# Buffers of a weight matrix split into high and low halves: four split blocks and four raw ones instead of five and two

## The chip, the cores and the metric

The kernel runs on one core of a Trainium2 chip. The metric is the device time of one execution in microseconds (us); lower is better. The engines are named as the profile names them: PE is TensorE, DVE is VectorE, ACT is ScalarE, POOL is GpSimd and SP is SyncE, which here only starts transfers.

## What is computed

A table of 12500 items with 512 numbers each, 1024 users with 200 item ids each. For each user the table's rows of all valid ids (below 12500) are averaged, and the average is multiplied by a 512 x 12500 matrix W; a bias is added. In the reference, cut to what matters:

```
valid = sequence_ids < emb_table.shape[0]
seq_emb = emb_table[where(valid, sequence_ids, 0)] * valid[..., None]
denom = maximum(valid.sum(axis=1, keepdims=True), 1.0)
user_repr = seq_emb.sum(axis=1) / denom
logits = user_repr @ proj_w + proj_b
```

Most ids are invalid: they are drawn up to 109962, so a user has some 23 valid ones.

## The kernel before, in words

**Tiles.** The users are 8 tiles t of 128 (TILES). W is cut into 25 blocks of 500 columns, each 512 x 500 floats, 1000 KB, held as four pieces of 128 rows. A *unit* is one product: one user tile by one block of W, into one of six banks of PSUM (BANKS). Each factor is split into a high part that PE takes exactly in fp32r and a low rest, and a unit is 4 pieces x 3 products (high by high L649, high by low L650, low by high L651), 12 matmuls. There are 200 units.

**Blocks of W.** A block passes through `load_w` (SP, L194 to L197: one transfer into one of RAW buffers w_raw), `w_high` (ACT, L298 to L302: the rounded copy w_hi) and `w_low` (DVE, L473 to L479: the rest w_lo, in two instructions L476 and L478). w_hi and w_lo have SPLIT buffers. A load may start when w_lo of the block RAW earlier is made (L196). `w_high(q)` waits until the last product with block q - SPLIT is done (L300).

**Means.** For every user tile, DVE sorts the ids (`sort`, L378), POOL starts 26 indirect gathers (FAST) of one table row per user, called columns here, into a ring of 12 row buffers (ROWS), and one more gather for rests. Before a gather, ACT sets two row buffers to zero (`clear`, L286 to L296), which must wait until the two columns that lay there were added. The columns of tiles 0 and 1 are added by PE (`sum_column`, L605), those of tiles 2 to 7 by DVE (`add_column`, L421). DVE then forms the mean (`mean_of`, L453 to L466), PE transposes it (`turn`, L582, matmul L587), ACT and DVE split it (`mean_high` L304, `mean_low` L468).

**Order of the work.** The means come one after the other while products already run, so user tile t joins late: at load q = JOIN[t] (0, 8, 12, 15, 18, 20, 22, 24). When it joins, it first catches up on the blocks still on chip, SPLIT - 1 before load q, and then shares every further block. `start[t]` (L44) is the first block of tile t; what it missed is loaded again at the end, so there are LOADS = start[-1] + 25 loads. L46 to L58 write the list of units and from it first_unit and last_unit of each block and joined[t], the first unit of tile t. With SPLIT = 5: LOADS = 45 and joined = 0, 8, 20, 33, 49, 63, 79, 97. With SPLIT = 4 the same lines give LOADS = 46 and joined = 0, 8, 19, 31, 46, 59, 74, 91.

Every engine runs one loop over the units r. Two rules set what goes between:

```
split_due = [None] * SPLIT + [min(last_unit[q - SPLIT] + 1, first_unit[q] - 1) for q in range(SPLIT, LOADS)]
begin, end = (joined[t - 1] - MEAN_AHEAD + 1, joined[t] - SUM_AHEAD) if t >= ON_PE else (2, joined[t] - 2)
return begin + (end - begin) * j // (FAST - 1)
```

The first (L71) gives the unit at which block q is split: DVE does w_low(q) after moving out unit split_due[q], ACT does w_high(q) one unit earlier, and ahead of that unit's clears (L346 to L360). The second (L65 to L69, `column_due`) spreads the 26 columns j of tile t over the units ahead of its joining. For tile 1 (units 2 to 6, the same at either SPLIT) it gives columns 0 to 6 at unit 2, 7 to 12 at unit 3, 13 to 18 at unit 4, 19 to 24 at unit 5 and 25 at unit 6. Column 24 goes into the buffer that column 12 left, and the clear of that pair (12, 13) stands in ACT's list at unit 4. `mean_of(t)` stands on DVE after unit joined[t] - 3, `turn(t)` on PE before unit joined[t] - 1.

DVE also moves every unit out of PSUM and adds the bias (`move_out`, L481 to L490, instruction L489); a unit of PE waits until the unit six before it was moved. SP stores one or two units at a time.

The last due times, for the blocks that matter here. SPLIT = 5: blocks 5, 6, 7, 8 at units 1, 2, 3, 4, block 9 at 9. SPLIT = 4: blocks 4, 5, 6, 7, 8 at units 1, 2, 3, 4, 5, block 9 at 9. Before the first mean, ACT and DVE split blocks 0 to SPLIT - 1 (L331 to L337 and L536 to L555), and SP loads blocks 0 to SPLIT + RAW - 1, the first RAW of them without a wait (L213 to L218).

Of the kernel before, what the change touches and what calls it, by code (L numbers as in the profile page):

```python
# [5 lines left out]
def mean_embedding_projection(nc, ids, table, proj, bias, out, FAST=26,  # L6
# [17 lines left out]
    REST = SORTED - FAST  # L24
    REST_AT = 18
    LISTED = -(-FAST // TOP) * TOP
    RAW, SPLIT, BIAS, ROWS, PLACED, BANKS = 2, 5, 4, 12, 2, 6
    CH = 2
    ON_PE = 2
    COLS = FAST * TILES  # L30
# [23 lines left out]
    UNITS = len(units)  # L54
    assert UNITS == TILES * NB
    first_unit = [min(r for r, (x, _) in enumerate(units) if x == q) for q in range(LOADS)]
    last_unit = [max(r for r, (x, _) in enumerate(units) if x == q) for q in range(LOADS)]
    joined = [min(r for r, (_, x) in enumerate(units) if x == t) for t in range(TILES)]  # L58
    stores, at = [], 0
    for q, first, n in steps:  # L60
# [18 lines left out]
    with ctx:  # L79
# [283 lines left out]
        def _(dve):  # L363
# [14 lines left out]
            def sort(t, r):  # L378
                at = SORT_OPS * t
                if r == 0:  # L380
                    keys(key[:], t, s_sort, at)
                eight = top[:, t, TOP * r:TOP * (r + 1)]
                dve.max(eight, key[:]).then_inc(s_sort, 1)  # L383
                dve.wait_ge(s_sort, at + KEY_OPS + 2 * r + 1)
                dve.tensor_scalar(index[:, t, TOP * r:TOP * (r + 1)], eight, -1.0, float(ITEMS),
                                  ALU.mult, ALU.add).then_inc(s_index, 1)
                dve.match_replace(key[:], eight, key[:], -1.0).then_inc(s_sort, 1)  # L387
                dve.wait_ge(s_sort, at + KEY_OPS + 2 * r + 2)
# [64 lines left out]
            def mean_of(t):  # L453
                if t >= ON_PE:
                    dve.wait_ge(s_summed, FAST * (t + 1 - ON_PE))
                else:
                    if t:
                        dve.wait_ge(s_mean, t)
                    dve.memset(sums[:], 0.0).then_inc(s_cleared, 1)
                    dve.wait_ge(s_cleared, t + 1)  # L460
                add_further(t)
                if t:
                    dve.wait_ge(s_turned, t)
                dve.wait_ge(s_rest_mean, t + 1)
                dve.scalar_tensor_tensor(mean[:], sums[:], inv_count[:, t:t + 1], rest_mean[:], ALU.mult,  # L465
                                         ALU.add).then_inc(s_mean, 1)  # L466
# [6 lines left out]
            def w_low(q):  # L473
                dve.wait_ge(s_w_hi, q + 1)
                half = K // 2
                dve.tensor_tensor(w_lo[:, q % SPLIT, 0:half], w_raw[:, q % RAW, 0:half],  # L476
                                  w_hi[:, q % SPLIT, 0:half].bitcast(F32), ALU.subtract)
                dve.tensor_tensor(w_lo[:, q % SPLIT, half:], w_raw[:, q % RAW, half:],  # L478
                                  w_hi[:, q % SPLIT, half:].bitcast(F32), ALU.subtract).then_inc(s_w_lo, 1)  # L479
# [72 lines left out]
            w_low(3)  # L552
            for r in range(ROUNDS):
                sort(3, r)
            w_low(4)  # L555
            mean_of(0)
            mean_low(0)
            for r in range(UNITS):
# [116 lines left out]
```

## Time and profile before

| | |
|---|---|
| median of 3 runs | 692.52 us (692.03 to 693.82) |
| profiled execution, its own time | 696.46 us |
| its span, first to last instruction | 694.7 us |
| mean granted clock of PE | 0.963 of full speed |
| busy: PE, DVE, ACT, POOL | 628.5, 402.5, 206.4, 225.1 us |
| transfers | 157.61 MB, 227 GB/s over the span |
| chain that ended last, by engine | PE 69%, DVE 15%, DMA 6%, issue 6%, ACT 2% |

The span is shorter than the execution by what lies around it, 1.8 us. "Busy" is a sum over the whole span, in which the stages differ: in the first 53 us there is no product, until 409 us user tiles join one by one, and from there on only products run. In the timeline's rows the first number is the start in us, the second the duration, and brackets hold the idle time of the engine ahead of the instruction and what ended it. The waits' rows give the idle time in all, how many times, and the longest.

### The profile page before, as it was taken

How to read it: one execution, taken by the hardware profiler on the slowest of the kernel's cores; microseconds unless marked ns; L12 is line 12 of the kernel's file. 1: busy time of each engine (PE TensorE's matmuls, PEld its weight loads, DVE VectorE, ACT ScalarE, POOL GpSimd, SP SyncE). 2: the span in 40 equal slices, each digit the busy share in tenths (PEclk: the TensorE clock that was granted, in tenths of full speed). 3: DMA queues.
4: the chain of work that ended last, by engine and by line, in shares of the span. 5: the costliest groups of instructions: out<-in, count | busy, mean ns of one | idle time of the engine just before them, and what ended most of it. 6: DMA issues, size and time to landing. Idle time of an engine off the chain costs nothing.

```text
span 694.7 us, 7435 instructions
## 1 busy us (share of the span) xinstructions
PE 628.5 (90%) x2596; PEld 492.3 (71%) x2596; DVE 402.5 (58%) x733; ACT 206.4 (30%) x182; POOL 225.1 (32%) x227
## 2 busy tenths in 40 slices
PE   1968669974988998989999999999999999999998
PEld 0425336863866877868878878888888888888886
DVE  7973114987896988968658546433233444334342
ACT  6543243353554344335333022111111111112110
POOL 6773456456376376665736100000000000000000
PEclk9998879996997999999999999999999999999999
DMA  8976748798988988988869328745545555665753
GB/s 309 332 234 211 245 159 269 232 342 263 274 291 265 295 293 274 304 285 286 283 196 320 140 101 271 217 153 175 173 160 167 173 168 166 184 211 183 221 148 104
DMA packets 76251, 157.61 MB, mean 227 GB/s; under 512 B 8168, under 2 KB 63592, under 8 KB 76208
## 3 DMA queue, kind: packets, MB, share of 16 engines
q1 hardware_dynamic: 58928, 109.63, 47.9%
q0 software_dynamic: 17280, 47.47, 21.9%
q8 instruction: 20, 0.33, 0.2%
q14 instruction: 23, 0.19, 0.1%
HBM read 115.04 MB, written 51.20 MB: 239 GB/s over the span
## 4 chain that ended last, share of the span: by engine, by line
PE 69%; DVE 15%; DMA 6%; issue 6%; ACT 2%; DVEq 1%; POOL 0%; POOLq 0%; ACTq 0%
PE acc L651 22%; PE acc L649 21%; PE acc L650 21%; DVE sums L429 5%; PE turned L613 3%; DMA w_raw<-in_L_rec_proj_w_dram 3%; DMA rows<-in_L_rec_emb_table_dram,index 3%; DVE w_lo L478 2%; DVE w_lo L476 1%; DVE key L387 1%; ACT w_hi L302 1%; DVE top L383 1%; PE turned L587 1%; DVE stage L489 1%; DVEq L190 1%
## 5 line engine op out<-in xcount | busy, mean ns | idle before, releaser
L649 PE MATMUL acc<-w_hi,mean_hi 128*128 128x500 f32 x800 | 321.6, 402 | 1.4 <-DVE mean_lo L470 1.4
L651 PE MATMUL acc<-w_hi,mean_lo 128*128 128x500 f32 x800 | 317.6, 397 | 0.0
L650 PE MATMUL acc<-w_lo,mean_hi 128*128 128x500 f32 x800 | 314.9, 394 | 0.0
L489 DVE TENSOR_TENSOR stage<-acc,bias_sb 128x500 f32<-128x500 f32 x200 | 134.9, 676 | 237.2 <-PE acc L651 236.8
L252 POOL DMA_INDIRECT rows<-in_L_rec_emb_table_dram,index x208 | 215.6, 1036 | 155.9 <-ACT rows L295 85.9
L650 PEld LDWEIGHTS acc<-w_lo,mean_hi 128*128 128x128 f32 x800 | 153.5, 192 | 36.5 <-issue 3.2
L649 PEld LDWEIGHTS acc<-w_hi,mean_hi 128*128 128x128 f32 x800 | 153.5, 192 | 35.6 <-issue 3.2
L651 PEld LDWEIGHTS acc<-w_hi,mean_lo 128*128 128x128 f32 x800 | 152.8, 191 | 31.4
L302 ACT ACTIVATE w_hi<-w_raw 128x2000 fp32r<-128x2000 f32 x45 | 84.4, 1876 | 297.0 <-PE acc L651 258.8
L295 ACT ACTIVATE rows<-zero 128x1024 f32<-128x1024 f32 x104 | 107.2, 1050 | 112.4 <-DVE sums L429 88.7
L429 DVE TENSOR_TENSOR sums<-sums,rows 128x512 f32<-128x512 f32 x150 | 104.2, 695 | 6.1
L613 PE MATMUL turned<-rows,ident 128*128 128x512 f32 x104 | 52.8, 657 | 18.1 <-DMA rows<-in_L_rec_emb_table_dram,index 16.8
L476 DVE TENSOR_TENSOR w_lo<-w_raw,w_hi 128x1000 fp32r<-128x1000 f32 x45 | 53.8, 1196 | 11.5 <-ACT w_hi L302 11.4
L478 DVE TENSOR_TENSOR w_lo<-w_raw,w_hi 128x1000 fp32r<-128x1000 f32 x45 | 53.8, 1195 | 0.0
L613 PEld LDWEIGHTS turned<-rows,ident 128*128 128x128 f32 x104 | 21.0, 208 | 45.1 <-DMA rows<-in_L_rec_emb_table_dram,index 22.6
L587 PE MATMUL turned<-ident,mean 128*128 128x128 f32 x32 | 6.6, 340 | 29.6 <-DVE mean L465 29.6
L587 PEld LDWEIGHTS turned<-ident,mean 128*128 128x128 f32 x32 | 4.3, 169 | 33.1 <-DVE mean L465 33.0
L465 DVE SCALAR_TENSOR_TENSOR mean<-sums,inv_count,rest_mean 128x512 f32<-128x512 f32 x8 | 6.0, 751 | 18.6 <-issue 13.1
L383 DVE MAX8 top<-key 128x8 f32<-128x200 f32 x40 | 14.6, 366 | 0.8
L387 DVE MATCH_REPLACE8 key<-top,key 128x200 f32<-128x200 f32 x40 | 14.2, 355 | 0.0
L323 ACT ACTIVATE rest_mean<-turned,inv_count 128x512 f32<-128x512 f32 x8 | 5.4, 676 | 24.0 <-PE turned L603 19.8
L306 ACT ACTIVATE mean_hi<-turned 128x512 fp32r<-128x512 f32 x8 | 4.8, 598 | 23.4 <-PE turned L587 23.4
(67 smaller groups left out, 96.9 us busy)
## 6 DMA issues: line engine op xcount, KB each, us to landing
w_raw<-in_L_rec_proj_w_dram SPq DMA_DIRECT2D x45, 1000.0 KB, 6.0
out_dram<-stage SPq DMA_DIRECT2D x73, 500.0 KB, 4.4
out_dram<-stage SPq DMA_DIRECT2D x54, 250.0 KB, 3.3
bias_sb<-in_L_rec_proj_b_dram SPq DMA_DIRECT2D x45, 250.0 KB, 5.1
rows<-in_L_rec_emb_table_dram,index POOLq DMA_INDIRECT x208, 4.8
ids_sb<-in_r_sequence_ids_dram SPq DMA_DIRECT2D x1, 700.0 KB, 4.6
rest_rows<-in_L_rec_emb_table_dram,rest_index POOLq DMA_INDIRECT x8, 6.7
ids_sb<-in_r_sequence_ids_dram SPq DMA_DIRECT2D x1, 100.0 KB, 2.1
```

What stands on the lines that cost most here:

```text
L252: return pool.indirect_dma_start(out=dst, out_offset=None, in_=table, in_offset=bass.IndirectOffsetOnAxis(ap=column, axis=0), bounds_check ...
L295: nc.scalar.activation(rows[:, c % ROWS:c % ROWS + CH].rearrange("p c d -> p (c d)"), zero[:, 0:1].to_broadcast([P, CH * HID]), ACT.Copy). ...
L302: nc.scalar.activation(w_hi[:, q % SPLIT], w_raw[:, q % RAW], ACT.Copy).then_inc(s_w_hi, 1)
L383: dve.max(eight, key[:]).then_inc(s_sort, 1)
L429: dve.tensor_tensor(sums[:], sums[:], rows[:, c % ROWS], ALU.add).then_inc(s_summed, 1)
L476: dve.tensor_tensor(w_lo[:, q % SPLIT, 0:half], w_raw[:, q % RAW, 0:half], w_hi[:, q % SPLIT, 0:half].bitcast(F32), ALU.subtract)
L478: dve.tensor_tensor(w_lo[:, q % SPLIT, half:], w_raw[:, q % RAW, half:], w_hi[:, q % SPLIT, half:].bitcast(F32), ALU.subtract).then_inc(s_ ...
L489: dve.tensor_tensor(stage[:, g % STAGE, r - stores[g][0]], acc[:, r % BANKS, 0:BW], bias_sb[:, q % BIAS], ALU.add).then_inc(s_moved, 1)
L613: nc.tensor.matmul(turned[:], ident[:], rows[:, c % ROWS], start=j == 0, stop=j == FAST - 1).then_inc(s_added, 1)
L649: nc.tensor.matmul(bank, hi, high, start=k == 0, stop=False)
L650: nc.tensor.matmul(bank, hi, low, start=False, stop=False)
L651: last = nc.tensor.matmul(bank, lo, high, start=False, stop=k == K - 1)
```

## The change

Of the buffers, w_raw has four instead of two and w_hi and w_lo have four instead of five. A raw block takes 8 KB of a partition and a split one 16 KB, so both layouts take 96 KB. The split of block 4 ahead of the first mean is taken out of DVE's list; ACT's list follows from SPLIT, and so do the list of units, the due times and the number of loads.

```diff
-    RAW, SPLIT, BIAS, ROWS, PLACED, BANKS = 2, 5, 4, 12, 2, 6
+    RAW, SPLIT, BIAS, ROWS, PLACED, BANKS = 4, 4, 4, 12, 2, 6
...
             w_low(3)
             for r in range(ROUNDS):
                 sort(3, r)
-            w_low(4)
             mean_of(0)
             mean_low(0)
```

## Rows read from the trace of the kernel before

**Rows 1.** Windows from mean to mean: stretch, busy us (instructions), clock, DMA share, GB/s

```profile
0.00:53.09 53.09, 30.88 (x63) 12.88 (x63) 42.99 (x145) 30.44 (x29) 38.43 (x45) 0.97 0.86 294
...
116.85:165.42 48.57, 35.80 (x161) 29.06 (x159) 41.20 (x79) 23.14 (x22) 26.31 (x26) 0.90 0.88 285
```

**Rows 2.** Timeline of PE: the first transpose of the means of tiles 2, 3, 4, 5, 7

```profile
166.23 0.48 PE L587 MATMUL turned<-ident,mean 128*128 128x128 f32 x1 [13.58 <-DVE mean L465]
...
211.62 0.48 PE L587 MATMUL turned<-ident,mean 128*128 128x128 f32 x1 [6.22 <-DVE mean L465]
...
262.43 0.33 PE L587 MATMUL turned<-ident,mean 128*128 128x128 f32 x1 [2.26 <-DVE mean L465]
...
305.09 0.33 PE L587 MATMUL turned<-ident,mean 128*128 128x128 f32 x1 [2.47 <-DVE mean L465]
...
406.26 0.33 PE L587 MATMUL turned<-ident,mean 128*128 128x128 f32 x1 [1.02 <-DVE mean L465]
```

**Rows 3.** Waits of DVE in the stages of tiles 2, 3, 4, 6, 7, in turn

```profile
DVE w_lo L476 <- ACT w_hi L302: 2.0, 2, 1.1
...
DVE w_lo L476 <- ACT w_hi L302: 1.8, 1, 1.8
...
DVE w_lo L476 <- ACT w_hi L302: 1.3, 1, 1.3
...
DVE stage L489 <- PE acc L651: 10.5, 9, 2.2
...
DVE stage L489 <- PE acc L651: 14.0, 12, 2.4
```

**Rows 4.** Windows: units 97 to 199 (4 instructions of L650 a unit), of that line alone

```profile
409.48:691.40 281.92, 160.20 (x412) 77.62 (x412) 1.00 0.57 179
```

**Rows 5.** Timeline of ACT: the split of block 8, then clears

```profile
89.37 1.87 ACT L302 ACTIVATE w_hi<-w_raw 128x2000 fp32r<-128x2000 f32 x1 [11.30 <-PE acc L651]
91.15 5.76 ACT L295 ACTIVATE rows<-zero 128x1024 f32<-128x1024 f32 x6
```

**Rows 6.** Timeline of POOL: the gather of column 18 of tile 1

```profile
93.06 1.00 POOL L252 DMA_INDIRECT rows<-in_L_rec_emb_table_dram,index  x1 [7.20 <-ACT rows L295]
```

**Rows 7.** Timeline of PE: columns and starts of units 4 and 5 (two records a column)

```profile
99.27 2.08 PE L613 MATMUL turned<-rows,ident 128*128 128x512 f32 x2 [5.64 <-DMA rows<-in_L_rec_emb_table_dram,index]
100.36 1.41 PE L649 MATMUL acc<-w_hi,mean_hi 128*128 128x500 f32 x1
...
105.63 5.31 PE L613 MATMUL turned<-rows,ident 128*128 128x512 f32 x12
110.38 0.79 PE L649 MATMUL acc<-w_hi,mean_hi 128*128 128x500 f32 x1
```

**Rows 8.** Windows: units 32, 48, 62 (each after a join's wait), of L650 alone

```profile
212.39:217.54 5.15, 2.47 (x4) 1.33 (x4) 0.50 0.90 283
...
262.84:265.65 2.81, 1.55 (x4) 0.76 (x4) 1.00 0.84 270
...
305.50:309.87 4.37, 2.24 (x4) 1.08 (x4) 0.61 0.86 288
```

**Rows 9.** Timeline of DVE: the mean of tile 1; units 32 and 46 moved out

```profile
116.85 0.75 DVE L465 SCALAR_TENSOR_TENSOR mean<-sums,inv_count,rest_mean 128x512 f32<-128x512 f32 x1 [1.82 <-ACT rest_mean L323]
...
217.85 0.68 DVE L489 TENSOR_TENSOR stage<-acc,bias_sb 128x500 f32<-128x500 f32 x1 [2.35 <-PE acc L651]
...
257.48 0.68 DVE L489 TENSOR_TENSOR stage<-acc,bias_sb 128x500 f32<-128x500 f32 x1 [0.62 <-PE acc L651]
258.08 0.69 DVE L429 TENSOR_TENSOR sums<-sums,rows 128x512 f32<-128x512 f32 x1
```

**Rows 10.** The chain that ended last, by pieces, in the stage of tile 3

```profile
179.91 1.12 DVE w_lo L478
...
181.04 6.81 DMA w_raw<-in_L_rec_proj_w_dram
...
187.94 1.89 ACT w_hi L302
```

## The prediction

> **What bounds the kernel now.** I first cut the span where DVE forms a mean, since that is where the stages end; a window from one mean to the next shows which engine is full in it [rows 1]. Then I looked at PE ahead of each transposed mean: how long it stood, and for whom [rows 2]. Then at what DVE itself waited for between two means [rows 3], and at the stretch behind the last joining [rows 4].
>
> The reader is to see three regimes. Until the mean of tile 0 there is no product. From there to the last joining PE waits at every join for a mean of DVE: 13.58 us for tile 2, then 6.22, 2.26, 2.47 and, for tile 7, 1.02 [rows 2]. In the stages of tiles 2 to 5 DVE is the bound: it hardly waits for a product. In those of tiles 6 and 7 it waits for products 10.5 and 14.0 us [rows 3], so PE is the bound, and the small wait left at the join is the fixed way from unit joined - 3 through the last column to the mean. Behind the last joining only products run: 103 units in 281.92 us, 2.74 us each, with no gap [rows 4].
>
> So the end is the time of the mean of tile 7 plus all units not yet done by then. This is the ledger that I keep.
>
> **Part 1: what the list of units does.** Joins come at 8, 19, 31, 46, 59, 74, 91 instead of 8, 20, 33, 49, 63, 79, 97: the first stage keeps its 8 units and each of the six others loses one, since a tile catches up on three blocks, not four. The 200 units stay. Thus 6 units move behind the last joining: 6 x 2.74 = **+16.4 us** there. What must pay for them is a shorter way to each of the six means.
>
> **Part 2: stages of tiles 6 and 7, bound by PE.** Each loses a unit of PE: 2 x -2.74 = **-5.5 us**. DVE can follow: it has 10.5 and 14.0 us of waiting, and the stage shrinks for it by 2.74 less the 0.60 of one unit moved out.
>
> **Part 3: stages of tiles 2 to 5, bound by DVE.** DVE has the same 26 columns, sorts and splits in each (4, 3, 3 and 2 blocks fall due in them under either list), and one unit less to move out: from start to start 0.60 us [rows 9]. Besides, DVE's waits for a split whose block was late go away: 2.0, 1.8 and 1.3 us for tiles 2, 3, 4 [rows 3]; with four raw buffers the block of each split was asked for four splits earlier, many units before. Tile 4's stage also had a wait of 0.62 for product 46 [rows 9], which a PE one unit ahead takes away. That gives -2.6, -2.4, -2.5 and -0.6: **-8.1 us**. PE gets 2.74 earlier to each of these joins, so its wait there grows: nearly nothing for tiles 2 to 4, by 2.1 us for tile 5 (from 2.47 to 4.6). ACT's own waits for loads hide behind DVE's columns, which never wait for a gather in these stages, so they are worth nothing more.
>
> **Part 4: the stage of tile 1.** Its 8 units stay, and it isn't a matter of DVE: PE adds the columns itself and waits for gathers. Read the round at unit 3: ACT's split of block 8 has to wait for product 3 and starts at 89.37, the clears stand behind it (91.15) [rows 5], POOL's gather behind these at 93.06 [rows 6], it lands at 99.27 and unit 4 starts at 100.36 [rows 7]. From product to unit 10.99 us, though the columns alone need under 5. There are two such rounds, at units 2 and 3, because splits stand there ahead of clears. At unit 4 no split stood in ACT's list, and the next columns ran through: from 105.63 to unit 5 at 110.38 [rows 7]. Now block 8 moves to due time 5, that is to unit 4 of ACT, behind product 4 (it reuses block 4's buffers) and ahead of the clear that column 24 needs. So a third round: unit 5 starts at 105.83 + 10.99 = 116.8 instead of 110.38, **+6.4 us**. From below this is 0 (if the gather were early enough after all), from above 11.0; I take the value of the equal round just ahead of it. Then the clock: unit 4, behind a wait of 5.64, took 5.27 us (100.36 to 105.63) [rows 7] against 2.74 for a full-speed unit, so up to +2.5; unit 62, behind a shorter wait, took 4.37 [rows 8], so +1.6 from below. I take **+2.0**. Last, DVE splits block 8 behind unit 5, now ahead of the mean of tile 1: two instructions, of which the second takes 1.12 [rows 10], 2 x 1.12 = **+2.2 us**. The 1.82 us that DVE stood ahead of this mean [rows 9] could hide most of it; but the same pause stands ahead of other means whose sums are long ready, so it is the loading of registers, and the split comes on top. From below 0.4, from above 2.2. Sum of the stage: **+10.6 us**.
>
> **Part 5: before the first mean.** ACT's and DVE's split of block 4 goes, and two more loads (2 MB) are asked for at the start. At 294 GB/s two loads are 7.0 us of transfer. POOL's gathers follow each other there and PE's last columns wait for the last of them; DVE is done early. The loads could delay the first gathers by up to 7.0, or make the later ones faster because block 6's load has gone ahead. The first columns are no end of a chain, so I take **0**, from -1 to +2.3 (a third of the 7.0, as PE starts late on the first columns).
>
> **Part 6: the clock at joins.** Unit 32, behind a wait of 6.22, ran at 0.50, unit 48 behind 2.26 at 1.00, unit 62 behind 2.47 at 0.61 [rows 2, 8]. Tile 5's join will have 4.6 us of waiting: its next unit goes from 4.37 towards 5.15, **+0.8**. What tiles 2 to 5 lose otherwise is hidden in PE's waits. The Trainium skill (TensorE: Matmul & The Clock Gate, section "HAM oscillation — how this bites in real kernels") says that waits ahead of each piece of work let PE's clock fall to half each time, 1.2 instead of 2.4 GHz; by that rule tile 4's unit would be slow too, which at 2.26 us this trace does not show (clock 1.00); what it would cost is in the second rival.
>
> **Part 7: one more load, split and its parts.** 46 blocks instead of 45: the extra one falls behind the last joining, where DVE and ACT wait for PE, and has five units, 13.7 us, between due and use: nothing. Three stores fewer: nothing. If that cover were gone, 1.9 of ACT and 2.2 of DVE.
>
> **Sum.** 16.4 - 5.5 - 8.1 + 10.6 + 0 + 0.8 = **+14.2 us**. The profiled execution took 696.46 us (span 694.7 and 1.8 around it); by its own time the new one would take 710.7. It stands 3.9 us above the median of 692.52, so in terms of the median: **706.7 us**, slower by 2.1%.
>
> **Rivals.**
> - *No third round.* If the gather of column 24 is in time (ACT free early, or the clear not last), the 6.4 and 2.0 fall away: 706.7 - 8.4 = **698.3**. For it: other columns of unit 5 give 4.3 us of cover. Against: the rounds at units 2 and 3 have the same cover and stood.
> - *The clock and the early loads cost more.* If tile 4's join now also slows the next unit, DVE, which has few columns to do there, waits for it as it does for unit 32, 2.35 us [rows 9]; with the 2.3 of part 5: **711.4**.
> - *The loads of W were the bound* (the other side: not slower). The chain that ended last runs in tile 3's stage through a load of 6.81 and a split of 1.89 on ACT [rows 10]. Were these 8.7 us all to go from the way to the mean, instead of the 1.8 that DVE waited, stage 3 would gain until its PE has no more to wait, 5.5; stage 2 likewise 8.7 - 2.0 = 6.7; stage 4, where PE waits 2.5, some 1.5: 706.7 - 13.7 = **693.0**. It decides where DVE would have been done with everything ahead of that split. Against: DVE's own wait is 1.8, and it was busy 41.2 of 48.6 us in stage 2 [rows 1]. The Trainium skill (DMA: Bandwidth & Descriptors, section "Rules for kernel authors") says to issue a transfer early and wait late; that rule speaks for this case.
>
> **How the numbers follow.** The sum's case has 0.66, no third round 0.12, more clock and loads 0.11, loads as the bound 0.06; 0.05 is left for something unseen that makes it faster. A difference of 0.3% (2.1 us) is about what a measurement of this kernel can tell from none. Faster 0.05, same 0.06, slower 0.89. The range reaches from the case without a third round to the dear one: 698 to 712.
>
> **What would show it.** Right: the last joining comes at unit 91, with 109 units of 2.74 behind it; a third wait of PE of over 5 us for a gather, at about 110; splits on DVE that never wait for ACT; the mean of tile 1 some 10 us later, the gap of means 6 and 7 shorter by 2.7 each. Wrong: stages 2 to 5 shorter by more than 2.7 us each, or the stage of tile 1 unchanged. If stage 2 alone shrinks by 9 us, the chain of waits was right about the loads and I was not.

## The result, and the profile after

The changed kernel took 703.12 us (702.43 to 705.42, 4 runs) beside 693.17 us (692.03 to 694.47) for the kernel before: ratio 1.0149, 95% interval 1.0118 to 1.0179. It is slower by 1.5%, some 10 us. Its profiled execution took 703.12 us with a span of 701.4, the one of before 696.46 with 694.7; so the two traces differ by 6.7 us, and the profile of before happened to lie 3.3 us above its own median. On a later occasion all times were longer, and there the same change was faster; that is told with the experiments.

First the windows from mean to mean, cut as in [rows 1], now at the means of tiles 0 to 7 of the changed kernel (columns: the stretch, then its length, busy us of PE, PEld, DVE, ACT, POOL with their instructions, PE's clock, DMA share, GB/s):

```profile
0.00:51.19 51.19, 29.76 (x63) 11.35 (x63) 40.56 (x143) 28.92 (x28) 37.14 (x44) 1.00 0.94 331
51.19:123.02 71.83, 53.26 (x147) 32.46 (x147) 18.31 (x26) 24.09 (x23) 31.72 (x32) 0.83 0.62 193
123.02:168.84 45.82, 31.96 (x143) 26.00 (x143) 40.43 (x78) 22.44 (x21) 29.87 (x28) 0.91 0.92 320
168.84:212.84 44.00, 36.89 (x155) 30.02 (x155) 38.62 (x77) 20.78 (x20) 26.38 (x25) 0.89 0.85 285
212.84:260.54 47.70, 45.22 (x191) 36.92 (x191) 40.50 (x80) 20.90 (x20) 28.55 (x28) 0.94 0.89 288
260.54:301.48 40.94, 37.36 (x167) 30.52 (x167) 36.92 (x75) 19.04 (x19) 26.46 (x27) 0.99 0.90 290
301.48:348.79 47.31, 45.24 (x191) 36.95 (x191) 33.51 (x53) 19.25 (x19) 30.36 (x30) 0.94 0.86 282
348.79:398.01 49.22, 48.20 (x215) 39.53 (x215) 34.25 (x53) 12.50 (x12) 16.70 (x17) 1.00 0.62 209
398.01:701.40 303.39, 299.07 (x1324) 248.24 (x1324) 121.38 (x155) 40.03 (x22) 0.00 (x0) 1.00 0.54 170
```

The ledger of the prediction can be read off by subtracting the same stretches of before, whose means stand at 53.09, 116.85, 165.42, 210.82, 261.62, 304.29, 353.31 and 405.45 us:

| stretch | before | after | difference | forecast |
|---|---|---|---|---|
| to the mean of tile 0 | 53.09 | 51.19 | -1.9 | 0 |
| stage of tile 1 | 63.76 | 71.83 | +8.1 | +10.6 |
| tile 2 | 48.57 | 45.82 | -2.8 | -2.6 |
| tile 3 | 45.40 | 44.00 | -1.4 | -2.4 |
| tile 4 | 50.80 | 47.70 | -3.1 | -2.5 |
| tile 5 | 42.67 | 40.94 | -1.7 | -0.6 |
| tiles 6 and 7 | 101.16 | 96.53 | -4.6 | -4.7 |
| behind the mean of tile 7 | 289.25 | 303.39 | +14.1 | +16.4 |
| sum | 694.7 | 701.4 | +6.7 | +14.2 |

The forecast of tiles 6 and 7 is -5.5 of part 2 and the +0.8 of the clock behind tile 5's join, whose unit lies in that stretch.

The mean of tile 1 is 6.2 us later than before (123.02 for 116.85), that of tile 4 already 1.1 earlier and that of tile 7 7.4 earlier; then 6 more units stand behind it.

The third round of the stage of tile 1 is there. In the timeline of the changed kernel, ACT's split of block 8, the clear behind it, POOL's gather of column 24 and PE's wait for it (the lines of the changed file are one lower from L555 on: L612 is the old L613, L648 the old L649):

```profile
103.39 1.87 ACT L302 ACTIVATE w_hi<-w_raw 128x2000 fp32r<-128x2000 f32 x1 [11.59 <-PE acc L650]
105.17 1.04 ACT L295 ACTIVATE rows<-zero 128x1024 f32<-128x1024 f32 x1
...
107.06 0.99 POOL L252 DMA_INDIRECT rows<-in_L_rec_emb_table_dram,index  x1 [8.78 <-issue]
...
112.39 1.54 PE L612 MATMUL turned<-rows,ident 128*128 128x512 f32 x2 [4.74 <-DMA rows<-in_L_rec_emb_table_dram,index]
112.95 1.40 PE L648 MATMUL acc<-w_hi,mean_hi 128*128 128x500 f32 x1
```

It is the chain of [rows 5 to 7] once more, one unit later: from the split at 103.39 to unit 5 at 112.95 it is 9.56 us, where the round of unit 4 took 10.99. The split waited 11.59 us for its product, and the gather behind it landed 5.33 us after its start (6.21 in the round of unit 4).

PE's waits at the joins of tiles 2, 3, 4, 5 and 7, as in [rows 2]:

```profile
169.64 0.47 PE L586 MATMUL turned<-ident,mean 128*128 128x128 f32 x1 [13.86 <-DVE mean L465]
...
213.64 0.47 PE L586 MATMUL turned<-ident,mean 128*128 128x128 f32 x1 [7.11 <-DVE mean L465]
...
261.34 0.33 PE L586 MATMUL turned<-ident,mean 128*128 128x128 f32 x1 [2.48 <-DVE mean L465]
...
302.29 0.47 PE L586 MATMUL turned<-ident,mean 128*128 128x128 f32 x1 [3.59 <-DVE mean L465]
...
398.82 0.33 PE L586 MATMUL turned<-ident,mean 128*128 128x128 f32 x1 [1.03 <-DVE mean L465]
```

They were 13.58, 6.22, 2.26, 2.47 and 1.02. PE loses a unit in each stage and DVE's way to the mean shrinks by nearly as much, except in the stage of tile 5. DVE's waits in the stage of tile 2 (line, what it waited for, us in all, times, longest) no longer name a split:

```profile
DVE mean L465 <- issue: 4.4, 2, 2.8
DVE mean_lo L470 <- ACT mean_hi L306: 0.8, 1, 0.8
```

### The profile page after: what moved, and what is told of

Read it like the earlier page. It is cut to its first block, busy times and chain, and to the rows that moved or that the text cites. A ratio compares the mean times of both kernels' runs of the same rounds, so it can differ in the third digit from the quotient of the medians.

```text
span 701.4 us, 7435 instructions
## 1 busy us (share of the span) xinstructions
PE 627.0 (89%) x2596; PEld 492.0 (70%) x2596; DVE 404.5 (58%) x735; ACT 208.0 (30%) x183; POOL 227.2 (32%) x227
## 3 DMA queue, kind: packets, MB, share of 16 engines
q1 hardware_dynamic: 59552, 110.91, 47.4%
## 4 chain that ended last, share of the span: by engine, by line
PE 62%; DVE 18%; issue 10%; DMA 4%; POOL 2%; ACT 2%; DVEq 2%; POOLq 0%
PE acc L648 20%; PE acc L649 19%; PE acc L650 19%; DVE sums L429 8%; DMA rows<-in_L_rec_emb_table_dram,index 4%; DVE w_lo L476 2%; DVE w_lo L478 2%; POOL rows L252 2%; PE turned L612 2%; ACT rows L295 1%; DVE key L387 1%; DVE stage L489 1%; PE turned L586 1%; DVEq L190 1%; DVE mean L465 1%
## 5 line engine op out<-in xcount | busy, mean ns | idle before, releaser
L648 PE MATMUL acc<-w_hi,mean_hi 128*128 128x500 f32 x800 | 323.1, 404 | 1.4 <-DVE mean_lo L470 1.4
L649 PE MATMUL acc<-w_lo,mean_hi 128*128 128x500 f32 x800 | 315.1, 394 | 0.0
L650 PE MATMUL acc<-w_hi,mean_lo 128*128 128x500 f32 x800 | 314.5, 393 | 0.0
L648 PEld LDWEIGHTS acc<-w_hi,mean_hi 128*128 128x128 f32 x800 | 154.0, 193 | 35.7 <-issue 3.2
L649 PEld LDWEIGHTS acc<-w_lo,mean_hi 128*128 128x128 f32 x800 | 153.8, 192 | 33.6 <-issue 3.5
L650 PEld LDWEIGHTS acc<-w_hi,mean_lo 128*128 128x128 f32 x800 | 153.0, 191 | 31.9
L302 ACT ACTIVATE w_hi<-w_raw 128x2000 fp32r<-128x2000 f32 x46 | 86.2, 1874 | 297.5 <-PE acc L650 296.4
L612 PE MATMUL turned<-rows,ident 128*128 128x512 f32 x104 | 53.2, 648 | 21.7 <-DMA rows<-in_L_rec_emb_table_dram,index 20.3
L478 DVE TENSOR_TENSOR w_lo<-w_raw,w_hi 128x1000 fp32r<-128x1000 f32 x46 | 55.1, 1197 | 0.0
L476 DVE TENSOR_TENSOR w_lo<-w_raw,w_hi 128x1000 fp32r<-128x1000 f32 x46 | 54.9, 1193 | 0.1
L612 PEld LDWEIGHTS turned<-rows,ident 128*128 128x128 f32 x104 | 19.7, 201 | 49.9 <-DMA rows<-in_L_rec_emb_table_dram,index 31.6
L323 ACT ACTIVATE rest_mean<-turned,inv_count 128x512 f32<-128x512 f32 x8 | 5.4, 677 | 26.6 <-PE turned L602 17.9
```

Of the source, the lines that this page charges most:

```text
L302: nc.scalar.activation(w_hi[:, q % SPLIT], w_raw[:, q % RAW], ACT.Copy).then_inc(s_w_hi, 1)
L612: nc.tensor.matmul(turned[:], ident[:], rows[:, c % ROWS], start=j == 0, stop=j == FAST - 1).then_inc(s_added, 1)
L648: nc.tensor.matmul(bank, hi, high, start=k == 0, stop=False)
L649: nc.tensor.matmul(bank, hi, low, start=False, stop=False)
L650: last = nc.tensor.matmul(bank, lo, high, start=False, stop=k == K - 1)
```

## Experiments

Twelve runs were made: groups of four, four and three, and one alone, each group on one chip beside the kernel before. In the three groups the kernel before took 742.3, 735.1 and 739.7 us on the median, and beside the last run 728.4, not 693: the same program in a different setting. Ratios are to the kernel before of the same group.

**The kernel before once more**, for a trace of that setting.

> The kernel before, unchanged, for a second trace. My theory of the result: the first profile of before was some 3 us above its own median, and part of the shift by stages (mean of tile 0 at 53.1 against 51.2 us after the change) is scatter and not the change. Expected here: first mean at 51 to 53 us, units 97 to 199 again 2.74 us each. Rival: the first mean is always at 53.1 before the change, and its 1.9 us gain comes from the earlier loads and the split that left; then it stands at 53.1 here too.

It took 743.7 us, with the mean of tile 0 at 61.86. Units 97 to 199 took 2.736 us each, as before. What is longer stands ahead of the last joining. In its timeline, PE in the middle of a product, and DVE moving the unit ahead of it:

```profile
277.63 0.39 PE L650 MATMUL acc<-w_lo,mean_hi 128*128 128x500 f32 x1 [1.66 <-issue]
...
279.78 0.58 PE L651 MATMUL acc<-w_hi,mean_lo 128*128 128x500 f32 x1 [1.76 <-issue]
...
284.79 0.68 DVE L489 TENSOR_TENSOR stage<-acc,bias_sb 128x500 f32<-128x500 f32 x1 [11.39 <-remote]
```

PE's matmuls, otherwise 0.23 us apart, start 2.1 us apart, with 1.7 us of idle time between them and nothing that they wait for ("issue"), and DVE stands for 11.39 us with a releaser that is in none of this core's queues ("remote"), while POOL starts a gather every 1.30 us. I call these standstills. The three longest of DVE in this trace (11.4, 7.5 and 4.9 us) all end 2.4 to 2.8 us after the last gather of an unbroken row of POOL (that row ends at 282.1, 335.6 and 231.2 us); in the first trace of before POOL has such rows too, some of 20 gathers and more, without a standstill, so the rows alone don't make them. By the same cut as above, this run is longer than the first trace of before by 8.8 us ahead of the first mean and by 5.1, -0.7, 4.4, 13.6, 9.6, 4.0 and 2.4 in the seven stages, and by nothing behind them: 47.2 us. Neither theory on the first mean is tested by that, since it came even later than 53.1.

**The changed kernel in that setting.**

> The changed kernel, unchanged, beside the others of this call and a run of before on the same chip. In the call before this one the kernel before took 742 us, not 693, and its vector engine and PE stood still at places where the profile names no releaser in the core. Theory: in a calm setting the change costs 1.3 to 1.7%, as first measured; where those standstills are there, it goes by them and the sign may turn (variants of it ran at 725 against 742). Rival: the change always costs about 10 us, also where before takes 742.

It took 725.96 us, ratio 0.9891 (0.9821 to 0.9962): faster. Its windows for the stages of tiles 1, 4 and behind the last mean:

```profile
58.94:132.53 73.59, 54.43 (x147) 33.20 (x147) 18.41 (x26) 23.62 (x22) 29.12 (x29) 0.82 0.57 179
...
222.59:278.40 55.81, 46.79 (x191) 37.48 (x191) 40.62 (x80) 21.02 (x20) 30.45 (x31) 0.87 0.84 273
...
422.73:726.10 303.37, 299.07 (x1324) 248.26 (x1324) 121.38 (x155) 40.04 (x22) 0.00 (x0) 1.00 0.55 170
```

The last stretch is the same as in the first setting to 0.02 us, so the price of the 6 units is a fixed one. The standstills are there too, but the trace lost less to the setting: 726.1 - 701.4 = 24.7 us against the 47.2 of the kernel before. (These two traces are of different groups; by the medians within a group the kernel before lost 42 and 47 us, 735.1 and 739.7 for 693.2, and the changed kernel 23, 726.0 and 726.4 for 703.1.) In the stage of tile 4 it lost 8.1 us to the setting (55.81 for 47.70), the kernel before 13.6 (64.43 for 50.80). The difference, 22.5 us by the traces and 19 to 23 by the medians, is more than the 10 by which the change was slower: the sign turns.

**And once more.**

> The changed kernel beside the two below, for a third occasion. Theory: the ratio to before goes with the setting: 1.015 where before takes some 693 us, 0.98 to 0.99 where it takes 735 to 742 because the vector engine and PE stand still in the stages of tiles 0 and 4 to 7. Rival: it was drift between calls, and the ratio is on either side whatever before takes.

726.39 us, 0.9842 (0.9763 to 0.9920), beside 739.7. So far the ratio goes with the setting: 1.015 where before takes 693, below 1 where it takes 735 or 740. The first kind was met on one occasion only, so that half isn't repeated.

**Split blocks alone**: four of them, but two raw ones.

```diff
-    RAW, SPLIT, BIAS, ROWS, PLACED, BANKS = 4, 4, 4, 12, 2, 6
+    RAW, SPLIT, BIAS, ROWS, PLACED, BANKS = 2, 4, 4, 12, 2, 6
```

> Only one half of the change: four split blocks, but still two raw ones. Theory: the list of units and the third round before unit 5 come from the split blocks alone (units 4 to 5 again 15 us, 10 in the kernel before); the raw ones give back only what the vector engine waited for late blocks, 2.0 + 1.8 + 1.3 = 5.1 us. So 703.1 + 5.1 = 708 us. Rival 1: the loads of W were the bound of stages 2 to 4 and four raw buffers gave some 14 us: 717 us. Rival 2: raw buffers are worth nothing: 703 us.

736.95 us, 0.9969 (0.9918 to 1.0020). Units 4 to 5 took 16.3 us: the third round comes from the split blocks, as does the list of units. The kernel with four of both and w_raw elsewhere, in the same group (below), took 724.92, so two more raw blocks are worth 12.0 us in that setting, where I had 5.1. The two traces differ by more, 17.9 us. The stages of tiles 2 and 3 make 2.3 and 2.8 us of that, near the 2.0 and 1.8 of the prediction's part 3, though DVE's waits for a split in them are only 0.4 and 2.2; the stage of tile 4 makes 8.4 (63.24 against 54.87), by standstills that the trace does not tie to a load. All twelve traces of this setting bear the last one out: the stage of tile 4 takes 63.2 to 66.4 us in the five with two raw blocks (four of these with five split blocks, one with four) and 53.9 to 55.8 in the seven with four raw blocks. So that gain goes with the raw blocks, whichever the number of split ones. It is not the whole of the turned sign: with four split and two raw blocks the kernel is already no slower than before here (0.9969), and its stages of tiles 6 and 7 are 6.3 and 5.3 us shorter than those of the kernel before once more, where the first pair gave 1.7 and 2.9. In this setting "the loads of W were the bound" comes near in size (13.7); what it forecast for the stage of tile 2, 6.7 us less, is not there.

**The third round undone**: in ACT's list at unit 4 the split stands behind the clears.

```diff
                 for q in range(SPLIT, LOADS):
-                    if split_due[q] == r + 1:
+                    if split_due[q] == r + 1 and not (r == 4):
                         w_high(q)
...
                         clear(g + ring)
+                for q in range(SPLIT, LOADS):
+                    if split_due[q] == r + 1 and r == 4:
+                        w_high(q)
```

> The changed kernel with one step moved: in the scalar engine's list at unit 4 the split of block 8 stands behind the clears, not ahead of them. Theory: the third wait for a gather (4.74 us ahead of the last column of unit 5) goes, with the slow clock behind it: units 4 to 5 take 10 us instead of 15.2, unit 5 1.7 us less, so 703.1 - 6.8 = 696.3 us, and the mean of tile 1 comes that much earlier. Rival: the gather itself was late for another reason (full transfer queues), and the wait stays: 703.1.

724.99 us, against 724.92 for the kernel of the same group that keeps the round (the one with other places in memory, below). The round is gone: in this trace the last of the columns, the next unit, and then DVE moving unit 5:

```profile
115.02 1.02 PE L615 MATMUL turned<-rows,ident 128*128 128x512 f32 x2
115.48 0.80 PE L651 MATMUL acc<-w_hi,mean_hi 128*128 128x500 f32 x1
...
123.46 0.68 DVE L492 TENSOR_TENSOR stage<-acc,bias_sb 128x500 f32<-128x500 f32 x1 [9.56 <-PE acc L653]
```

Units 4 to 5 took 10.0 us and PE waited for no gather there (there: 16.0). But product 5 was done at 118.6, and DVE moved it only at 123.46: a standstill of some 5 us took the gain. The run shows the cause of the round, not its price.

**The same again.**

> The same kernel as in the earlier call, where the third wait for a gather went (units 4 to 5: 10.0 against 16.0 us in its sister) but the time did not fall, since the vector engine then stood still for some 5 us ahead of the mean of tile 1 with no releaser. Theory: without such a standstill the whole falls by the 6.8 us of the third round, against the changed kernel of this call. Rival: something else holds the mean of tile 1, and the time stays within 2 us of the changed kernel's.

725.2 us against 725.96 of the changed kernel in the group; units 4 to 5 in 8.7 us instead of 14.9, and again DVE stood still ahead of the mean of tile 1 (11.3 us "remote" in this stage). The rival has it by the time, in this setting alone; the four runs spread from 716 to 730 us, so a gain of some us would be hard to see. What the round costs without a standstill is shown only by the first pair of traces.

**Other places in memory**: w_raw allocated behind w_lo instead of ahead of w_hi.

```diff
-        w_raw = sb("w_raw", [P, RAW, K, BW], F32)
         w_hi = sb("w_hi", [P, SPLIT, K, BW], F32R)
         w_lo = sb("w_lo", [P, SPLIT, K, BW], F32R)
+        w_raw = sb("w_raw", [P, RAW, K, BW], F32)
```

> The changed kernel with the same work, only w_raw placed behind w_hi and w_lo in the memory, so that both of these lie 32000 bytes lower. In the traces a unit takes 2.72 to 2.75 us before the change, by which buffer its block lies in, and 2.70 to 2.73 after it. Theory: the place of w_hi and w_lo sets this, so the times per buffer change here (by 0.01 to 0.05 us each, and the whole by up to 200 x 0.03 = 6 us either way). Rival: it goes by something else (the number of buffers, what else runs), and units stay at 2.71 on the mean and the whole at 703.1.

724.92 us, and units as in the changed kernel to 0.001 us: 2.714, 2.708, 2.700 and 2.729 for the four buffers. The place as such changes nothing. But in the run with two raw blocks, where w_hi begins 16000 bytes lower, the same four times come rotated by two buffers: 2.700, 2.728, 2.714, 2.709. A buffer is 8000 bytes, that is 64 more than a whole number of 256. A shift of four buffers (32000, a whole number of 256) changes nothing and one of two buffers (128 more than such a number) rotates the times by two, so they fit the start's remainder by 256. What differs between four and five buffers is that with five the matching w_lo starts 40000 bytes behind w_hi, 64 off.

**That distance, in the kernel before**: the stage buffers (24000 bytes) between w_hi and w_lo, which makes it 64000.

```diff
         w_hi = sb("w_hi", [P, SPLIT, K, BW], F32R)
+        stage = sb("stage", [P, STAGE, GROUP, BW], F32)
         w_lo = sb("w_lo", [P, SPLIT, K, BW], F32R)
         bias_sb = sb("bias_sb", [P, BIAS, BW], F32)
-        stage = sb("stage", [P, STAGE, GROUP, BW], F32)
```

> The kernel before with the same work, only the stage buffers placed between w_hi and w_lo in the memory, so that w_lo lies 64000 bytes behind w_hi and not 40000. In all traces with four split blocks w_lo lies 32000 bytes behind w_hi, a whole number of 256, and a unit takes 2.713 us on the mean, wherever the pair lies; with five the distance is 64 bytes off such a number and it takes 2.736. Theory: the distance sets it, and units 97 to 199 take 2.71 here, 200 x 0.023 = 4.6 us less over all or at least the 2.4 of the last stretch. Rival: it goes by the number of split blocks, and they stay at 2.74.

The windows of the units behind the last joining, of the instructions of L649 alone (stretch, length, PE and PEld busy, clock, DMA share, GB/s). The kernel before, its units 97 to 199:

```profile
409.48:691.40 281.92, 160.07 (x412) 77.22 (x411) 1.00 0.57 179
```

The same 103 units with the stage buffers between:

```profile
454.10:733.30 279.20, 160.06 (x412) 77.20 (x411) 1.00 0.58 180
```

2.710 us a unit instead of 2.736, with five split blocks. By buffer they take 2.700, 2.729, 2.714, 2.709 and 2.700 us, the times of the run with two raw and four split blocks, where w_hi starts at the same place, with the fifth like the first; before it was 2.752, 2.727, 2.726, 2.720 and 2.748. So the distance sets it, not the number of blocks, and it gives 2.7 us here. (The step also moves the stage and bias buffers, but from the kernel before to the changed one these stay where they were and the unit still goes from 2.736 to 2.713.) The whole took 738.36, ratio 1.0037 (0.9957 to 1.0117): too small to be seen in that setting.

**Splits behind clears in the kernel before**, in the whole stage of tile 1 (the diff of the third round with `r < joined[1]` for `r == 4`).

> The kernel before (five split blocks, two raw), with one step moved: in the stage of tile 1 the scalar engine's splits stand behind its clears. Theory: the rounds of product, split, clear, gather at units 2 and 3 go as the third one does; both waits of PE for a gather (5.7 and 5.6 us) and the slow clock behind them vanish, units 2 to 5 take some 8.5 us each instead of 14.4, 15.9 and 10.0, so 12 to 15 us less than the kernel before. Rival: the gathers are then paced by their own issue (1.30 us each) or their landing and PE waits as before: 0 to 3 us less.

726.22 us, 0.9882 (0.9822 to 0.9941). PE waits for no gather any more; units 2 to 5 start 7.9 us apart, and the stage takes 47.7 us instead of the 68.9 of the kernel before once more. By the medians within the group 9 us arrive, between the theory's 12 to 15 and the rival's 3. Against the trace once more, which is of another group, 17 us are left (741.9 to 724.9): the next stage takes back 3.5, and every other is within 1.1. The group has no trace of the kernel before itself, so where the rest of its gain goes is not shown.

**The same in the changed kernel.**

> The changed kernel with the scalar engine's splits behind its clears in the whole stage of tile 1. In the kernel before, this step took the stage from 68.9 to 47.7 us. Theory: here all three waits for a gather go, the stage falls from some 73 to 48 us and the whole by 18 to 25 us against the changed kernel (some comes back in the next stage, where the clears then have no lead): about 703 us where the changed kernel takes 726, 682 where it takes 703. Rival: the next stages take it all back, since the gathers then bound them: within 5 us of the changed kernel.

707.03 us, 0.9585 (0.9506 to 0.9664) of before, 0.973 of the changed kernel in its group. Its windows for the stages of tiles 1 and 2:

```profile
58.09:109.51 51.42, 46.78 (x147) 29.21 (x147) 18.28 (x26) 24.05 (x22) 26.26 (x26) 0.91 0.71 226
109.51:156.60 47.09, 33.75 (x143) 27.12 (x143) 40.65 (x77) 22.31 (x21) 32.73 (x30) 0.88 0.95 340
```

And PE's columns ahead of units 3, 4 and 5, which follow their unit without a wait:

```profile
78.87 5.31 PE L615 MATMUL turned<-rows,ident 128*128 128x512 f32 x12
...
86.75 5.31 PE L615 MATMUL turned<-rows,ident 128*128 128x512 f32 x12
...
94.61 5.31 PE L615 MATMUL turned<-rows,ident 128*128 128x512 f32 x12
```

The stage of tile 1 falls from 72.8 us to 51.4 in the group, and the next one keeps its length (47.4 and 47.1). 19.4 us arrive. So the three rounds together, not the work of splitting W, which is still there, were the large cost of this stage. This version beats both kernels in this setting; in the one of the first pair it wasn't run.

**Both steps in the kernel before.**

> The kernel before with both steps: splits behind clears in the stage of tile 1, and the stage buffers between w_hi and w_lo. Theory: they add up, 9 to 17 us of the first and 2 to 5 us of the second: 0.965 to 0.985 of the kernel before, units 97 to 199 at 2.71 us each. Rival: the second is lost in standstills, as when it stood alone (1.004): 0.98 to 0.99 and still 2.71 us a unit in the last stretch.

715.61 us, 0.9719 (0.9630 to 0.9808), units at 2.710 us. In this setting five split blocks with both steps stay behind four with one; the stage of tile 4 alone is 65.3 us against 55.0, as in the other traces with two raw blocks against four.

**The split of block 8 behind the mean**, on top of the best version.

```diff
                 for q in range(SPLIT, LOADS):
-                    if split_due[q] == r:
+                    if split_due[q] == r and r != joined[1] - MEAN_AHEAD:
                         w_low(q)
...
                     mean_of(joined.index(r + MEAN_AHEAD))
+                for q in range(SPLIT, LOADS):
+                    if split_due[q] == r and r == joined[1] - MEAN_AHEAD:
+                        w_low(q)
```

> The changed kernel with the splits behind the clears in the stage of tile 1 (0.9585 of before in the last call), and besides the vector engine's split of block 8 behind the mean of tile 1, not ahead of it. Theory of the prediction: this split costs 2.2 us ahead of that mean, so the way from the move of unit 5 to the mean gets 2.2 us shorter, and the whole by up to 2 us: about 0.955 of before. Rival: the split stood beside a wait for registers and products and costs nothing there, or comes back ahead of the next mean, whose stage the vector engine bounds (then the first way is 2.2 shorter, the next stage 2.2 longer, and the ratio stays at 0.958).

704.69 us, 0.9670 (0.9616 to 0.9723), beside a kernel before of 728.4; the ratio can't be held against the 0.9585 of another setting, so on the whole this is open. The way is clear from the traces: from the start of unit 6 to the mean of tile 1 it is 3.0 us instead of 5.7, which is the 2.2 of the split and 0.5 that was not traced, and the next stage is 47.3 instead of 47.1, so nothing is taken back there.

## Why the prediction was right, and where its terms were off

It forecast 706.7 us and a range of 698 to 712; measured were 703.1. The sign, the mechanism and the order of the terms held in the setting that it was made for: 6 units behind the last joining, a third round in the stage of tile 1, and six shorter ways to a mean that don't pay for them. The size is less well met than the 3.6 us between 706.7 and 703.1 say. The ledger compares two traces, and there 14.2 us were forecast and 6.7 measured, with most terms too dear. The forecast for the median comes nearer because it takes off the 3.9 us by which the trace of before lay above its median; those us lie somewhere in the stages of that trace, and part of what the ledger missed is them (1.7 are found below, ahead of the first mean). By its steps:

- **The units behind the last joining**: 16.4 forecast, 14.1 measured. The number of units was right. The duration was not the same on both sides: I took 2.74 us for all 109, and they take 2.71, since the distance of w_lo from w_hi changed with the number of buffers. 109 x 0.023 = 2.5 us. No row of before could say that; but durations from 2.72 to 2.75 by buffer were to be seen and I had averaged over them.
- **The third round**: 6.4 forecast, 5.1 measured (units 4 to 5 in 15.16 us instead of 10.02), mostly as this gather landed 0.9 us sooner; the wait for it was 4.74 us, a little under the "over 5" that was to show it. The clock behind it: 2.0 against 1.7 (unit 5 to 6: 6.07 for 4.42). The split of block 8 ahead of the mean: 2.2 against 2.0 (from unit 6 to the mean 4.0 us instead of 2.05), so it did come on top of DVE's pause, which is still 1.56. The rounds at units 2 and 3 were 0.5 us shorter besides.
- **Stages of tiles 2 to 4**: 7.5 forecast, 7.3 measured. DVE's waits for a split are gone. Tile 3's stage gave 1.0 less, of which 0.5 is DVE's longer wait for the slow unit behind the join of tile 2 (0.91 for 0.41). "Shorter by more than 2.7 each" was to show the forecast wrong: tiles 2 and 4 pass it narrowly (2.8 and 3.1), tiles 3 and 5 don't (1.4 and 1.7).
- **Stage of tile 5**: 0.6 forecast, 1.7 measured; PE's wait is 3.59 and not 4.6. Of the 1.1 more, 0.3 is the loading of registers; the rest was not traced.
- **The clock at the joins**: behind 2.48 us of waiting the transpose took 0.33 us, as before behind 2.26; behind 3.59 it took 0.47, as one at the lower level does. So tile 4's join kept its clock (its unit took 2.80 us), against the second rival. The unit behind tile 5's join took 4.85 us for 4.36, so the 0.8 is 0.5. Waits of 2.47 us, before, and 2.48, after, lie on either side: the first let the clock fall within the unit, the second didn't, and no run here says why. The rule of the Trainium skill that the prediction set beside it (TensorE: Matmul & The Clock Gate, "HAM oscillation — how this bites in real kernels") agrees with the traces at waits of 3.59 us and more here, not at 2.48. The prediction put that rule more widely than the page does, whose kernel waits longer than tile 4's join at each step; so this join does not speak against the page.
- **Before the first mean**: 0 forecast, 1.9 us less measured. The range went to -1. Both chains run through the same gather, started at 39.44 us before and 39.23 after, so 0.2 is that. The rest is PE's last columns and the product between them: before, behind a wait of 3.58 us, they ran at the lower level (granted clock 0.68 from 45.99 to 51.39 us), after, behind one of 1.42, at full clock (1.00 over the same stretch). Whether the change or scatter made the waits shorter is open: in the other setting the first mean comes at 52.2 to 61.9 us in the five traces with two raw blocks and at 57.2 to 61.4 in the seven with four.
- **The rivals**: no third round and the dear clock did not come. Loads as the bound: by the first pair of traces no, stage 2 gained 2.8 and not 9.

What the prediction did not have at all is the setting. Its numbers stand on a kernel at 693 us; at 735 to 740 us the change is 1.1 to 1.6% faster, because the setting costs it 19 to 23 us less. That the loss is smaller with four raw blocks is shown for the stage of tile 4 (8.4 us in one group, with no overlap between the five traces with two raw blocks and the seven with four); what starves PE and DVE there is open. The groups ran on different chips at different times, and no run here could tell a chip apart from an hour.

## What to carry to other kernels

Where an engine's list mixes work that waits for a product with work that frees buffers for a transfer, put the freeing first: in the stage of tile 1 that alone was worth 19 us in the changed kernel and 9 in the kernel before, both in the slower setting, where two more raw blocks gave 12. A count of buffers that also sets a schedule moves waits to places that have nothing to do with the buffers; write both lists of due times out, and look at what stands ahead of what. And a time of two kernels in one setting is a result for that setting.

## What was not expected of the hardware

- The time of a unit of 12 matmuls at full clock depends on where the two moving operands start against each other: 2.710 to 2.713 us on the mean when w_lo starts 32000 or 64000 bytes behind w_hi, both whole numbers of 256, and 2.736 at 40000, which is 64 off. Other distances were not tried. Within each layout single buffers differ by up to 0.03, and the pattern fits the start's remainder by 256. Why is open.
- The same program took 693 and 742 us on different occasions, with the stretch behind the mean of tile 7, nearly all pure products, equal to 0.04 us (289.25 and 289.21) and all of the difference in stretches in which gathers, loads and DVE run together. There DVE stood up to 11.4 us and PE up to 1.8 us between two matmuls of a unit, without a releaser.
